# An attention and feed-forward kernel whose feed-forward output is built with features on partitions

## What is computed

```python
x1 = x + attn_out                       # attn_out = softmax(q k^T) v @ wo, 16 heads of 128
h2 = _rms_norm(x1, ln2_w)
mlp = jax.nn.silu(h2 @ w_gate) * (h2 @ w_up) @ w_down
processed = x1 + mlp
gate = jax.nn.sigmoid(sel_scores).reshape(S, 1)
gated = gate * processed + (1.0 - gate) * x
output = hidden_states.at[b, idx].set(gated.reshape(B, k, D))
```

## Time and profile before

| | us |
|---|---|
| three runs | 1722.62, 1723.48, 1725.57 (median 1723.48) |
| the profiled execution | 1722.89 |
| its span in the trace | 1721.2 |

### The profile page before, as it was taken

How to read it: one execution, slowest core, us unless ns; L and a number is a source line. 1 busy time by engine, 2 the same in 40 slices (tenths; PEclk the granted TensorE clock), 3 DMA queues, 4 the chain that set the end, 5 groups by cost and what they waited for, 6 DMA issues and landing times.

```text
span 1721.2 us, 43831 instructions
## 1 busy us (share of the span) xinstructions
PE 1607.0 (93%) x17669; PEld 1223.5 (71%) x17669; DVE 1098.0 (64%) x1751; ACT 688.8 (40%) x1406; POOL 679.1 (39%) x758
## 2 busy tenths in 40 slices
PE   5778999999999999999999999999984998998997
PEld 4556677777777777777777777777762886644886
DVE  4543477767676767677666777676763756632766
ACT  4555344434434443444344444344332216511331
POOL 4553244444344434443443444443433760010542
PEclk9999999999999999999999999999996999998999
DMA  5633111211121111211121112111127104002000
GB/s 177 196 104 80 49 52 46 74 54 50 45 71 57 50 45 62 66 45 50 52 76 45 50 45 73 55 50 45 53 90 260 57 1 196 1 0 98 1 1 22
DMA packets 66103, 113.71 MB, mean 66 GB/s; under 512 B 21328, under 2 KB 36016, under 8 KB 64512
## 3 DMA queue, kind: packets, MB, share of 16 engines
q1 hardware_dynamic: 65216, 110.20, 20.2%
q0 software_dynamic: 832, 2.75, 0.6%
HBM read 82.59 MB, written 30.34 MB: 66 GB/s over the span
## 4 chain that ended last, share of the span: by engine, by line
PE 87%; DVE 5%; POOL 4%; ACT 2%; issue 1%; DMA 1%; DVEq 0%; POOLq 0%; ACTq 0%; SPq 0%
PE ps L1207 19%; PE ps L1209 16%; PE ps L1208 16%; PE ps L1334 11%; PE ps L1309 7%; PE ps L1500 3%; PE ps L1259 3%; PE ps L1282 3%; PE ps L1484 2%; PE ps L1312 1%; PE ps L1465 1%; POOL xa L469 1%; PE ps L1222 1%; DVE xT_lo L894 1%; POOL tile_var L463 1%
## 5 line engine op out<-in xcount | busy, mean ns | idle before, releaser
L934 DVE RECIPROCAL rec<-ps 128x224 f32<-128x224 f32 x128 | 199.2, 1556 | 95.2 <-PE ps L1334 92.6
L495 POOL TENSOR_TENSOR prob_img<-prob 128x448 f32<-128x448 f32 x128 | 157.4, 1230 | 234.5 <-PE ps L1334 212.9
L458 POOL TENSOR_TENSOR ctx_lo<-ctx_raw,ctx_hi 128x472 fp32r<-128x472 f32 x64 | 115.3, 1821 | 288.7 <-ACT ctx_hi L639 288.7
L696 ACT ACTIVATE prob<-ps 119x448 f32<-119x448 f32 x128 | 69.6, 544 | 248.3 <-PE ps L1312 248.3
L929 DVE TENSOR_REDUCE top<-ps 112x4 f32<-112x1028 f32 x128 | 156.2, 1220 | 0.0
L1309 PEld LDWEIGHTS ps<-q_all,k_all 32*128 32x128 f32 (+1 forms) x3072 | 120.9, 185 | 39.6 <-issue 31.4
L1309 PE MATMUL ps<-q_all,k_all 32*128 32x112 f32 (+1 forms) x3072 | 147.2, 299 | 1.4 <-ACT prob L698 1.4
L928 DVE TENSOR_REDUCE top<-ps 112x4 f32<-112x472 f32 x128 | 83.0, 649 | 83.6 <-PE ps L1282 83.6
L672 ACT ACTIVATE sq_junk<-proj 128x513 bf16<-128x513 f32 (+1 forms) x96 | 61.1, 637 | 183.3 <-DVE proj L908 183.3
L698 ACT ACTIVATE prob<-ps 128x896 f32<-128x896 f32 x128 | 116.8, 912 | 0.0
L615 POOL TENSOR_TENSOR ring_lo<-ring,gate_up_hi 128x512 fp32r<-128x512 f32 x32 | 42.2, 1343 | 169.8 <-ACT gate_up_hi L850 169.8
(11 more groups left out here) (293 smaller groups left out, 4372.5 us busy)
## 6 DMA issues: line engine op xcount, KB each, us to landing
ctx_raw<-in_ctx_dram SPq DMA_DIRECT2D x32, 748.0 KB, 4.2
xh_dram<-xh SPq DMA_DIRECT2D x32, 448.0 KB, 3.1
xa<-in_x_dram SPq DMA_DIRECT2D x28, 256.0 KB, 2.8
q_dram<-q_turned SPq DMA_DIRECT2D x28, 256.0 KB, 2.7
q_all<-q_dram SPq DMA_DIRECT2D x32, 224.0 KB, 3.1
xh<-in_x_dram SPq DMA_DIRECT2D x32, 224.0 KB, 2.9
out_dram<-out_sb SPq DMA_DIRECT2D x32, 224.0 KB, 2.3
ring<-in_wq_dram SPq DMA_DIRECT2D x1, 4096.0 KB, 14.0
```

Of the source, the lines that this page charges most:

```text
L458: nc.gpsimd.tensor_tensor(ctx_lo[:, :, cols], ctx_raw[:, :, cols], ctx_hi[:, :, cols].bitcast(F32), ALU.subtract).then_inc(ctx_lo_done, 1)
L495: nc.gpsimd.tensor_tensor(prob_img[:], prob[:, g % 2, 1, :], prob[:, g % 2, 2, :], ALU.add).then_inc(img_summed, 1)
L934: nc.vector.reciprocal(rec[:], bank[:, 2:4]).then_inc(norm_step, 1)
```

## The change

The output of attention and of the MLP is built transposed, with features on partitions, and turned back at the end.

- The output projection is no longer a stage. `output_T(h)` is called inside the attention loop, two heads behind the scores: for each of four feature blocks an `mm3` of 448 columns, with `wo` stationary (high part rounded by ACT in `wo_rounded`, low part subtracted by POOL), in banks 0 to 3. The attention of a head is split as well: ACT rounds it (`attn_rounded`), DVE subtracts (`attn_lo`). At head 0 sixteen small float32 matmuls add the residual.
- Banks 0 to 3 are then taken, so the scores alternate between banks 4 and 5 where they had four, the transposes have bank 6 alone, and `weigh` bank 7 alone. `turn_probs(k)` waits for the copy of block k - 1.
- The gate is computed between the additions of the values' bias, and its scratch is `rows4`. DVE therefore first waits for the last `rotate`.
- The second norm squares on ACT, sums over partitions by 16 float32 matmuls with a column of ones, turns the root into a row with four PE transposes, and scales and splits block by block; the first gate matmuls start as blocks arrive.
- `down(j)` has the weights stationary: 12 matmuls of 448 columns where there were 12 of 512.
- At the end DVE adds the residual by feature block, PE turns sixteen blocks back, and DVE mixes by the gate.
- `w_down` is loaded in four quarters as `wo` is used up.

```diff
-                if k >= 2:
-                    pe.wait_ge(pT_ready, k - 1)
+                if k:
+                    pe.wait_ge(pT_ready, k)
+                else:
+                    pe.wait_ge(val_ready, 2 * NC)
                 for b in range(c + 1):
-                    last = nc.tensor.transpose(ps[0:L, 4 + k % 2, b * L:(b + 1) * L], prob2[:, k % (LAG + 1), b * L:(b + 1) * L], ident[0:L, 0:L])
+                    last = nc.tensor.transpose(ps[0:L, 6, b * L:(b + 1) * L], prob2[:, k % (LAG + 1), b * L:(b + 1) * L], ident[0:L, 0:L])
...
+            def output_T(h):
+                pe.wait_ge(attn_ready, h + 1)
+                pe.wait_ge(w_lo_done, FH + FKV + 2 + h + 1)
+                for kc in range(KC):
+                    cols = slice(kc * P, (kc + 1) * P)
+                    last = mm3(ps[:, kc, 0:S], wo_hi[:, h % 2, cols], wo_lo[:, h, cols], attn_hi[:, h, :], attn_lo[:, h % 2], h == 0, h == FH - 1)
+                    if h == 0:
+                        for c in range(NC):
+                            last = nc.tensor.matmul(ps[:, kc, c * L:(c + 1) * L], xh_sel[:, c, 1, cols], ident[0:L, 0:L], start=False, stop=False)
...
-            for k in range(FH * NC + LAG + 2):
+            for k in range(FH * NC + 2 * LAG + 1):
                 if k < FH * NC:
                     att(k)
                 if LAG <= k < FH * NC + LAG:
                     turn_probs(k - LAG)
-                if k > NC + LAG and (k - LAG) % NC == 1:
-                    weigh((k - LAG) // NC - 1)
-            pe.wait_ge(ring_loaded[2], 16)
-            pe.wait_ge(attn_ready, FH)
+                if k % NC == 0 and k >= 2 * NC:
+                    weigh(k // NC - 2)
+                if k % NC == 2 and k >= 2 * NC + 2:
+                    output_T(k // NC - 2)
+            for kc in range(KC):
+                pe.wait_ge(mid_squared, kc + 1)
+                for c in range(NC):
+                    last = nc.tensor.matmul(ps[0:L, 4 + c, 0:1], mid_sq[:, kc, c * L:(c + 1) * L], ones_col[:], start=kc == 0, stop=kc == KC - 1)
+            last.then_inc(sums_full, 1)
+            pe.wait_ge(rstd_ready, 2)
             for c in range(NC):
-                for h in range(FH):
-                    last = nc.tensor.matmul(ps[0:L, c, :], attnT[:, h, c * L:(c + 1) * L], wo[:, h, :], start=h == 0, stop=h == FH - 1)
-                last.then_inc(mid_full, 1)
-            turn_tokens(1)
+                last = nc.tensor.transpose(ps[:, 7, c * L:(c + 1) * L], rstd[:, c:c + 1].to_broadcast([L, P]), ident[0:L, 0:L])
+            last.then_inc(root_row_full, 1)
...
+            dve.wait_ge(head_ready, FH + FKV)
+            gate_junk = rows4[0:L].rearrange("l a s -> l (a s)")[:, 0:D]
...
-                for c in range(NC):
-                    cols = slice(c * L, (c + 1) * L)
-                    last = mm3(ps[0:L, 4 + c, :], m_hi[:, j % 2, cols], m_lo[:, j % 2, cols], down_hi[:, j % 3], w_down_lo[:, j, :],
-                               j == 0, j == FC - 1)
+                for kc in range(KC):
+                    cols = slice(kc * P, (kc + 1) * P)
+                    last = mm3(ps[:, kc, 0:S], down_hi[:, j % 3, cols], w_down_lo[:, j, cols], m_hi[:, j % 2, :], m_lo[:, j % 2, :], j == 0, j == FC - 1)
...
             for c in range(NC):
-                dve.wait_ge(down_full, c + 1)
-                nc.vector.tensor_tensor(x_mid[:, c], ps[0:L, 4 + c, :], x_mid[:, c], ALU.add).then_inc(sum_ready, 1)
-                dve.wait_ge(sum_ready, c + 1)
-                nc.vector.scalar_tensor_tensor(keep[:, c], x_mid[:, c], gate[:, c:c + 1], keep[:, c], ALU.mult, ALU.add).then_inc(final_ready, 1)
+                dve.wait_ge(turned_back, c + 1)
+                nc.vector.scalar_tensor_tensor(keep[:, c], ps[0:L, 4 + c, :], gate[:, c:c + 1], keep[:, c], ALU.mult, ALU.add).then_inc(final_ready, 1)
```

More of the change, by code:

```diff
@@ L609, in _ @@
                 rotate(h)
+            for h in range(FH):
+                pool.wait_ge(w_hi_done, FH + FKV + 2 + h + 1)
+                nc.gpsimd.tensor_tensor(wo_lo[:, h, :], wo[:, h, :], wo_hi[:, h % 2].bitcast(F32), ALU.subtract).then_inc(w_lo_done, 1)
             def gate_up_rest(j):
@@ L859, in _ @@
[L859 to L867, removed]
+                if k % NC == 2 and 1 <= k // NC <= FH:
+                    wo_rounded(k // NC - 1)
@@ L1155, in _ @@
-            nc.vector.reciprocal(gate[:], gate_e[:]).then_inc(gate_step, 1)
-            dve.wait_ge(gate_step, NC + 2)
-            nc.vector.tensor_scalar(gate_e[:], gate[:], -1.0, 1.0, ALU.mult, ALU.add).then_inc(gate_step, 1)
-            dve.wait_ge(gate_step, NC + 3)
-            for c in range(NC):
-                last = nc.vector.scalar_tensor_tensor(keep[:, c], xh_sel[:, c, 1], gate_e[:, c:c + 1], xh_sel[:, c, 0], ALU.mult, ALU.add)
-            last.then_inc(gate_step, 1)
-            for c in range(NC):
-                dve.wait_ge(mid_full, c + 1)
-                nc.vector.tensor_tensor(x_mid[:, c], ps[0:L, c, :], xh_sel[:, c, 1], ALU.add).then_inc(mid_ready, 1)
@@ L1165, in _ @@
[L1165 to L1172 removed]
+                h = k // NC - 2
+                if k % NC == 1 and h >= 0:
+                    dve.wait_ge(attn_hi_done, h + 1)
+                    if h >= 2:
+                        dve.wait_ge(o_step, h - 1)
+                    nc.vector.tensor_tensor(attn_lo[:, h % 2], ps[:, 7, 0:S], attn_hi[:, h, :].bitcast(F32), ALU.subtract).then_inc(attn_ready, 1)
@@ new lines, in _, with mid_rest @@
+            for kc in range(KC):
+                at = FH + FKV + KC + kc
+                dve.wait_ge(mid_squared, kc + 1)
+                nc.vector.tensor_scalar(mid_normed[:, kc, :], ps[:, kc, 0:S], fvec[:, at:at + 1], None, ALU.mult).then_inc(mid_scaled, 1)
+            dve.wait_ge(root_ready, 2)
+            nc.vector.reciprocal(rstd[:], rstd[:]).then_inc(rstd_ready, 1)
+            dve.wait_ge(root_row_full, 1)
+            def mid_rest(kc):
+                dve.wait_ge(hT_hi_done, KC + kc + 1)
+                nc.vector.tensor_tensor(hT_lo[:, kc, :], mid_normed[:, kc, :], hT_hi[:, kc, :].bitcast(F32), ALU.subtract).then_inc(hT_ready, 1)
@@ L1174, in hidden_rest @@
+            for kc in range(KC):
+                dve.wait_ge(mid_scaled, KC + kc)
+                nc.vector.tensor_tensor(mid_normed[:, kc, :], mid_normed[:, kc, :], ps[:, 7, 0:S], ALU.mult).then_inc(mid_scaled, 1)
+                if kc:
+                    mid_rest(kc - 1)
+            mid_rest(KC - 1)
             def hidden_rest(j):
@@ L1529, in _ @@
                     down(j - 2)
+            for kc in range(KC):
+                pe.wait_ge(processed_ready, kc + 1)
+                for c in range(NC):
+                    last = nc.tensor.transpose(ps[0:L, 4 + c, kc * P:(kc + 1) * P], processed[:, kc, c * L:(c + 1) * L], ident[:])
+                    if kc == KC - 1:
+                        last.then_inc(turned_back, 1)
 def kernel(**inputs):
```

203 lines of the change are left out of this document (133 added, 70 removed).

## The result

The changed kernel takes 1730.45 us (median of six runs, 1728.27 to 1733.55), the kernel before 1723.59 (six runs, 1722.62 to 1725.57). The ratio is 1.004, 95% interval 1.0027 to 1.0053: slower by 4.6 to 9.1 us. The forecast was 1730.0. The profiled execution of after took 1733.55 us with a span of 1731.8, 10.6 more than the 1721.2 of before.

What follows compares the result with a forecast made beforehand. From 1419.96 us on, PE's work or waits of PE were taken to bound every stage but the second norm. Terms summed to +6.4 us, execution 1722.9 to 1729.3; with 0.6 for the median, 1730.0, range 1717 to 1740.

Steps and rivals of the forecast that it cites:

- first layer, not touched: Everything before 1400 us: taken as untouched by the change, so no term in the sum.
- start: Values before the first head: DVE's first addition waits for POOL's last rotation, delaying PE's third group of value matmuls, +2.5 us.
- first eight steps: First steps of attention: nothing covers the chain from scores to copy, 10.9 against 8.94 us, +1.9.
- heads with the residual: Fourteen heads at 9.70 us (work 7.44, waits 1.53 and 0.73), +55.4; sixteen float32 residual matmuls at head 0, +3.0.
- projection: Output projection after attention: the separate stage goes, -55.2 us.
- end of attention: After head 14's weighing: last transposes, products, weighing, rounding, subtracting and twelve matmuls take 11.9 against 6.36 us, +5.6.
- second norm: Between projection and MLP: first gate matmul 6.7 us after the projection, later blocks at DVE's pace, -3.5 us.
- MLP: Down products drop from 2.77 to 2.42 us each, one of sixteen hidden by a growing wait, -5.2 us.
- end: After the last matmul: turning back and mixing, then POOL's pace sets the scatters, fourth at +6.0 against +4.1, +1.9 us.
- The rival that the wait doesn't grow: Two transposes in each head: ACT late by a fixed amount, wait stays 0.71, head 8.15 us, total 1708; chance 0.12.
- break-even of 9.24: Period of a head in us: above it the kernel is slower; under it the prediction is wrong.
- PE's clock falls: Values or first steps: one or two falls, about 2.6 us each, 1732.5 to 1735, chance 0.17; half clock throughout, 1803, 0.02.

Runs made afterwards that it cites:

- copy-first: The kernel after, with ACT's copy of the transposed block of step k-3 ahead of the exponential of step k: 1706.65 us, ratio to before 0.9907.
- weighing-first: The kernel after, with PE's weighing ahead of the two transposes at a head's first step, ACT unchanged: 1710.73 us, ratio to before 0.993.
- before with the copy first: The kernel before, with ACT's copy of step k-3 ahead of the exponential of step k: 1713.82 us, ratio to before 0.9939.
- a bank taken away: The kernel before with all transposes in one bank: 1750.66 us with ACT's exponential ahead of its copy, 1723.30 us with the copy ahead.
- the kernels of this study that start alike and kept the clock: The kernel after with ACT's copy ahead of the exponential (1706.65 us), weighing ahead of two transposes (1710.73), or six output products in heads 1 to 14 (1712.12).
- the products ahead of the transposes: The kernel after with ACT's copy ahead of the exponential, gate scratch over the cosine table, and PE's twelve output products ahead of the four transposes: 1719.98 us.

## Why the prediction was right, step by step

I take each term from the same two marks in the profiles of before and after.

| term | forecast | measured | how |
|---|---|---|---|
| first layer, not touched | 0 | +2.3 | DVE's last rotation at 1399.47, then at 1401.77 |
| start | +2.5 | +4.3 | 24.75 against 20.49 |
| first eight steps | +1.9 | +1.8 | 10.73 against 8.94 |
| heads with the residual | +58.4 | +59.9 | 140.28 against 80.36 |
| projection | -55.2 | -55.2 | gone |
| end of attention | +5.6 | +5.5 | 11.90 against 6.36 |
| second norm | -3.5 | -5.5 | to the end of the first 24 gate and up products: 13.23 (1589.43 to 1602.66) against 18.71 (1570.82 to 1589.53) |
| MLP | -5.2 | -4.9 | from there to the last matmul: 118.54 against 123.44 |
| end | +1.9 | +2.4 | 10.60 against 8.23 |
| sum | +6.4 | +10.6 | |

**Heads: right, by the mechanism forecast.** The chain of scores, maximum, exponential, copy gave the first wait as 1.53; the starts show 1.54 (1448.79, with 0.05 for the causal add, to 1450.38). The second came as 0.74 for 0.73, the first eight steps as 10.73 for 10.9. The period is about 9.76 for 9.70, the twelve products taking 2.51 (1454.93 to 1457.44) for 2.42. Of the 1.5 us that the term lacked, 0.9 is that period, and 0.6 the residual, 3.6 for 3.0 (its head took 13.34, 1437.25 to 1450.59). That ACT's place in the chain is the cause was only argued there; the copy-first and weighing-first kernels show it.

**The rival that the wait doesn't grow** fell, as the period of 9.76 is above its break-even of 9.24. What it stood on, ACT late by a fixed amount, is refuted by before with the copy first. The rule of the Trainium skill's "Perfetto Trace Analysis" (Optimization Strategy), that a repeated gap can mean too little PSUM for the next tile, is half borne out: a bank taken away cost 27.2 us with the exponential first and 9.5 with the copy first, but the 0.71 of before went with the banks as they were.

**Start: mis-sized, 2.5 for 4.3.** The stop of PE was right: 2.64, from 1405.72, where the third group of value products would have stood, to 1408.37. The rest is the clock, at 0.57 from 1408 to 1412 us: eight products at 0.43 for 0.23 us, +1.6. This was the rival "PE's clock falls", at the first of the places named, for 1.6 rather than 2.6. It came in addition to the forecast's own mechanism, and the kernels of this study that start alike and kept the clock show that it need not come.

**Second norm: mis-sized, -3.5 for -5.5.** The first gate product came 6.86 us after the projection (6.7 forecast). The first twelve products ended 11.4 us after the projection for 10.9. I had them follow DVE's pace; the rows show no wait for DVE behind the first product, but half clock for the first eight. And I had put the second twelve at half clock throughout, 4.3 us, where full clock was back and they took 1.8:

```profile
1596.29 0.71 PE L1278 MATMUL ps<-hT_hi,gate_up_hi 128*128 128x448 f32 x1 [2.07 <-DVE hT_lo L1234]
...
1599.05 0.55 PE L1279 MATMUL ps<-hT_lo,gate_up_hi 128*128 128x448 f32 x1
1599.42 0.38 PE L1280 MATMUL ps<-hT_hi,ring_lo 128*128 128x448 f32 x1
```

**MLP: right.** The period is 7.28 (gate products at 1616.41, 1623.69, 1630.97) for 7.27. DVE was busy 4.6 and 5.2 us of these two periods, a little less than the 5.4 that the prediction gave it.

**End: right in kind, 0.5 short.** POOL's pace sets it, at 1.25 for 1.22, and the last issue comes 6.5 us after the last matmul for 6.0:

```profile
1722.89 2.73 DVE L1272 SCALAR_TENSOR_TENSOR xh_sel<-ps,gate,xh_sel 112x512 f32<-112x512 f32 x4 [0.86 <-PE ps L1625]
1723.92 0.99 POOL L656 DMA_INDIRECT out_dram<-xh_sel,tok  x1 [12.21 <-DVE xh_sel L1272]
...
1727.72 0.94 POOL L656 DMA_INDIRECT out_dram<-xh_sel,tok  x1 [0.30 <-issue]
```

**What made the total fit better than the profile does.** The terms that the change touches sum to +8.3, not 6.4, and the profiled execution of after was the slowest of its six. The first layer, the same in all kernels, ended (DVE's last rotation) between 1397.4 and 1402.6 us in the twelve profiles of this study, so 2.3 of the 10.6 are no effect of the change. The medians differ by 6.9. That the forecast lies 0.5 from the median is thus partly luck: errors of +1.8, +1.5 and +0.5 stand against one of -2.0.

## What to carry to other kernels

Where two kinds of work share an engine's in-order queue, one that is ready early (a copy of something just made) and one that waits for a chain (an exponential behind a maximum), the order of the two is worth as much as a buffer: try it before spending a bank, and look again once a buffer has been taken away. A wait on such a chain is its length less the work the waiting engine has of its own before it ends; a wait that falls while the chain runs shortens the one at its end. And an order that is right with one partner turns wrong when the partner's order changes, as the products ahead of the transposes showed: trace every queue around both ends.

## What was not expected of the hardware

- The granted clock fell in two executions and not in three others after the same stop of PE of 2.44 to 2.48 us, at a point where the programs are the same. It cost 1.2 to 1.6 us each time. The Trainium skill's page "TensorE: Matmul & The Clock Gate" (HAM oscillation) tells of longer waits, one in each pass of a loop, that send the matmuls back to the half clock every time; here the waits of 1.37 us in the heads never did (granted clock 1.00), and the one of 2.5 us did twice in five.
- DVE's four mixings in the work on the gate (112x512 each, from two SBUF tensors) took 5.78 us in before, where POOL's subtractions ran beside them from 1519.64 on, and 2.74 in after, where POOL stood still. The page "GPSIMD Engine Reference" of the Trainium skill (Specifications) says that the two share their interface to SBUF, so that a DVE instruction with two SBUF inputs can meet contention; the rows agree, and no run isolated it. At 2.74 us they fit beside a group of value products (12 x 0.231 = 2.77); that they would have delayed the values at 5.78 is an estimate that no run shows.

```profile
1519.18 5.78 DVE L1160 SCALAR_TENSOR_TENSOR xh_sel<-xh_sel,gate_e 112x512 f32<-112x512 f32 x4
```

```profile
1421.98 2.74 DVE L1200 SCALAR_TENSOR_TENSOR xh_sel<-xh_sel,gate_e 112x512 f32<-112x512 f32 x4
```
